# Two layers of AdaLN attention and mixture of experts: the group norm's Newton steps and the decay's affine step change engines in the first attention

## The chip, the cores and the metric

The kernel runs on one core of a Trainium2 chip. The engines that matter here are TensorE (PE in the profile), VectorE (DVE), ScalarE (ACT), GpSimd (POOL) and SyncE (SP), which issues most of the transfers. The metric is the device time of one execution, in microseconds; lower is better. Three runs of the kernel before took 1299.35, 1291.67 and 1298.77 us, so the median is 1298.77.

## The reference, cut to what matters

Two layers work on `x` of 8 sequences, 512 tokens, 128 features. Each layer is `x + ga * attention(h)` and then `x + gb * ffn(h)`, where `h` is a layer norm of `x` with a scale and a shift per sequence. The first layer's attention is a linear recurrence over time with 16 heads of 8 features, and the change lies in it alone:

```python
dd = sigmoid(tanh(einsum('btd,ed->bte', x_shift, ddlerp_w)))
r, k, v = proj(lerp(mix_r), r_w), proj(lerp(mix_k), k_w), proj(lerp(mix_v), v_w)
g = silu(proj(lerp(mix_g), g_w))
w = -softplus(-proj(lerp(mix_w), w_w)) - 0.5
# per step: state = state * exp(w_t) + k_t v_t ;  o_t = sum_v state * r_t
out = _wkv_scan(r, k, v, w)
mu, var = out.mean(-1), out.var(-1)             # over the 8 features of a head
out = (out - mu) / sqrt(var + GN_EPS) * gn_weight + gn_bias
return einsum('btd,ed->bte', out * g, out_w)
```

The decay `exp(w)` is `exp(-0.5) * sigmoid(z)` with `z` the projection, which the kernel computes as `0.5 * exp(-0.5) * (tanh(z/2) + 1)`. The rest (mixture of experts, windowed and global attention, second mixture) is not touched.

## The kernel before

The stage of the first attention works on one sequence at a time, as 128 features x 512 tokens, in a software pipeline. `recurrent_rows` (line 384) runs `step(i)` for i from -3 to 10 on every engine's own queue, with a list of parts written out by hand; in `step(i)` the letters are n = i+3, m = i+2, a = i+1, b = i-1, c = i-2, d = i-3. So in one step sequence i is scanned, sequence i+1 gets its projections, sequence i-1 gets its head norm, output projection and second layer norm, sequence i-2 goes through the shared expert and the router, and i-3 is scattered to the expert slots. Every engine takes its parts strictly in the written order, and semaphores tie the engines together.

**The scan.** For each of the 8 value features j, `unit(b, j)` on DVE multiplies the keys by a row of `vrow` (line 916) and runs the scan with the decay tile `decs[b % 2]` (line 918). `received(b, j)` on POOL multiplies the result with `rrow` (line 1311), and `accumulate(b, j)` on TensorE adds it up, less the head's mean, in PSUM bank 7 (line 1973). `vrow` and `rrow` are values and receptions spread over the partitions: SP stores `vS` (line 482) and `rS` (line 487) to DRAM and loads them back broadcast, 4 MB a sequence (`load_rows`, line 499), in the order units 0 to 3, 6 and 7, 4 and 5. The loads of units 0 to 3 for sequence i+1 wait for both stores and for the accumulation of unit 3 of sequence i. In SP's order `store_reception` and `load_rows` stand behind `load_gate`, which waits for POOL's `gated_shared` (line 1323).

**The head norm.** ScalarE squares and copies bank 7 (lines 1571 and 1572). At the end of step i, `head_variance(i)` on DVE reduces the squares and makes the first guess of the reciprocal root with integer operations on `gnr` (128x64, lines 932 to 935). In step i+1 POOL begins with `head_rsqrt(b)`: three Newton steps of four operations (lines 1336 to 1339), each waiting for the one before by the semaphore `a_gn`. DVE's `head_norm(b)` (line 942) waits for the sixteenth count. It stands behind `unit(i, 0)`, the router of sequence c and `unit(i, 1)`. Then TensorE transposes the heads (`heads_T`, line 1890), ScalarE scales them (`scale_heads`, line 1588), POOL multiplies them with the gate (`gated_y`, line 1349), and TensorE projects (`attended`, lines 2014 and 2020). POOL's own order in a step is `head_rsqrt(b)`, `received(i, 0)`, `scatter` of d (line 1275, four indirect transfers), `gated_out`, `gated_y`, `received` 1 to 3, `gated_shared`, `received` 4 and 5, the second norm's scale, `received` 6, `decay(a)`, `received` 7, `scatter` of c, and the scales of the first and third norm.

**The decay.** ScalarE's `decay(b)` (line 1559) takes the tanh out of bank 2; POOL's `decay(a)` (line 1304) adds 1 and multiplies by `DECAY` in place, for the first `unit` of the next step. On ScalarE the gate's tanh follows (line 1565), then the router's exponential (line 1580), the first modulation (line 1506) and the copy of the attended sequence (line 1592).

ScalarE also issues three transfers: `load_gate`, `load_second` (line 1520, the sequence's residual, which waits for the store of the sequence two before) and `store_second` (line 1525). `load_second` stands ahead of `scale_heads` and of the key's copy (line 1547), which TensorE's next projections need. `keep_busy` (line 1885) is filler on TensorE, around the last sequence.

Of the kernel before, what the change touches and what calls it, by code (L numbers as in the profile page):

```python
# [18 lines left out]
ALU = mybir.AluOpType  # L19
ACT = mybir.ActivationFunctionType  # L20
# [21 lines left out]
DECAY = 0.5 * 0.6065306597126334  # L42
# [16 lines left out]
def build(nc, io):  # L59
    nc.disable_value_cache = True  # L60
    with ExitStack() as ctx:
# [58 lines left out]
        dT, tT, eT, aT_, _, _, vS, kS, dec, gs, tg, y1 = (rows[:, i, :] for i in range(12))  # L120
# [32 lines left out]
        kSs, decs = (kS, late[:, 2, :]), (dec, late[:, 3, :])  # L153
# [16 lines left out]
        gnr = sb("gnr", [P, 3, NT * H])  # L170
# [54 lines left out]
        S = Semaphores()  # L225
# [109 lines left out]
        def ok(b):  # L335

            return 0 <= b < NB

        def half_of(q):

            return q // 2 % 2, q % 2
# [54 lines left out]
        def settled(eng):  # L396

            eng.sem_inc(S["settled"], 1)
# [211 lines left out]
        def _(v):  # L610
            V = nc.vector
# [309 lines left out]
            def head_variance(b):  # L921

                n = [0]

                def link(ins):
                    n[0] += 1
                    ins.then_inc(S["a_gn"], 1)
                    if n[0] < 4:
                        v.wait_ge(S["a_gn"], b * 16 + n[0])
                gv, gy = gnr[:, 0, :], gnr[:, 1, :]  # L930
                v.wait_ge(S["a_sq"], 2 * b + 2)
                link(V.tensor_reduce(gv, sq.rearrange("p (a c) -> p a c", c=DH), axis=AX, op=ALU.add))
                link(V.tensor_scalar(gv, gv, 1.0 / DH, GN_EPS, ALU.mult, ALU.add))
                link(V.tensor_scalar(gy.bitcast(I32), gv.bitcast(I32), 1, None, ALU.logical_shift_right))
                link(V.tensor_scalar(gy.bitcast(I32), gy.bitcast(I32), -1.0, float(RSQRT_MAGIC), ALU.mult, ALU.add))

            def head_norm(b):

                v.wait_ge(S["a_gn"], b * 16 + 16)
                if b:  # L940
                    v.wait_ge(S["a_onT"], b)
                V.tensor_tensor(on.rearrange("p t (h c) -> p (t h) c", c=DH),
                                accS.rearrange("p (a c) -> p a c", c=DH), bc(gnr[:, 1, :], DH, 2), ALU.mult).then_inc(S["a_on"], 1)
# [20 lines left out]
            def step(i):  # L964
                n, m, a, b, c = i + 3, i + 2, i + 1, i - 1, i - 2
                if ok(i):
                    unit(i, 0)
                if ok(c):
                    router(0, c, ROUTE_EPS, 0)
                if ok(i):  # L970
                    unit(i, 1)
                if ok(b):
                    head_norm(b)
                if ok(c):
                    shared_product(c, 0)
                if ok(i):
                    unit(i, 2)
                    unit(i, 3)
                    unit(i, 4)
                    unit(i, 5)  # L980
                if ok(a):
                    gate(a)
                if m == 0:
                    mod_columns()
                    prepare()
                if ok(m):
                    shift(m)
                if ok(b):
                    stats_second(b)
                if ok(c):  # L990
                    router(0, c, ROUTE_EPS, 1)
                if ok(i):
                    unit(i, 6)
                    unit(i, 7)
                if ok(c):
                    place(0, c)
                    shared_product(c, 1)
                if ok(n):
                    stats_first(n)
                if ok(m):  # L1000
                    lerp(m)
                if m == 0:
                    mod_rows()
                    prepare_rest()
                if ok(b):
                    stats_third(b)
                if ok(i):
                    head_variance(i)
# [225 lines left out]
        def _(p):  # L1234
            G_ = nc.gpsimd
# [62 lines left out]
            def norm_second(b):  # L1298
                ln_scale_less("ln2_st", "ln2_rs", b, veps, mv, rstd, nb2)

            def decay(a):
                p.wait_ge(S["a_tz"], a + 1)
                settled(p)
                G_.tensor_scalar(decs[a % 2], decs[a % 2], 1.0, DECAY, ALU.add, ALU.mult).then_inc(S["a_dec"], 1)

            def received(b, j):

                p.wait_ge(S["a_scan"], b * DH + j + 1)
# [13 lines left out]
                    p.wait_ge(S["b_y"], c)  # L1322
                G_.tensor_tensor(swg, wshd[:, :, :], bc(mgd, FC, 1), ALU.mult).then_inc(S["a_swg"], 1)

            def head_rsqrt(b):

                n = [4]

                def link(ins):
                    n[0] += 1  # L1330
                    ins.then_inc(S["a_gn"], 1)
                    p.wait_ge(S["a_gn"], b * 16 + n[0])
                gv, gy, ga_ = gnr[:, 0, :], gnr[:, 1, :], gnr[:, 2, :]
                p.wait_ge(S["a_gn"], b * 16 + 4)
                for _ in range(3):
                    link(G_.tensor_tensor(ga_, gy, gy, ALU.mult))
                    link(G_.tensor_tensor(ga_, ga_, gv, ALU.mult))
                    link(G_.tensor_scalar(ga_, ga_, -0.5, 1.5, ALU.mult, ALU.add))
                    link(G_.tensor_tensor(gy, gy, ga_, ALU.mult))

            def norm_third(b):
                if b:
                    p.wait_ge(S["r_sorted"], b)
# [6 lines left out]

            def step(i):
                n, a, b, c, d = i + 3, i + 1, i - 1, i - 2, i - 3
                if ok(b):
                    head_rsqrt(b)
                if ok(i):
                    received(i, 0)
                if ok(d):
                    scatter(0, d, 1)
                if ok(b):
                    gated_out(b)  # L1360
                    gated_y(b)
                if ok(i):
                    received(i, 1)
                    received(i, 2)
                    received(i, 3)
                if ok(c):
                    gated_shared(c)
                if ok(i):
                    received(i, 4)
                    received(i, 5)  # L1370
                if ok(b):
                    norm_second(b)
                if ok(i):
                    received(i, 6)
                if ok(d):
                    scattered(0, d)
                if ok(a):
                    decay(a)
                if ok(i):
                    received(i, 7)  # L1380
                if ok(c):
                    scatter(0, c, 0)
                if ok(n):
                    norm_first(n)
                if ok(b):
                    norm_third(b)
# [78 lines left out]
        def _(a):  # L1465
            A = nc.scalar
# [88 lines left out]
            def decay(b):  # L1555
                a.wait_ge(S["a_z"], b + 1)
                if b >= 2:
                    a.wait_ge(S["a_scan"], (b - 1) * DH)
                A.activation(decs[b % 2], bank[2][:, :], ACT.Tanh, scale=0.5).then_inc(S["a_tz"], 1)

            def gate_tanh(b):
                a.wait_ge(S["a_g"], b + 1)
# [305 lines left out]
            for q in range(HALVES - 4, HALVES):  # L1868
                p, h = half_of(q)
# [686 lines left out]
```

## Time and profile before

| | us |
|---|---|
| median of three runs | 1298.77 |
| the profiled execution | 1300.29 |
| its span, first to last instruction | 1298.5 |
| TensorE busy | 1151.7 (89%) |
| DVE busy | 834.5 (64%) |
| ScalarE busy | 504.0 (39%) |
| POOL busy | 597.1 (46%) |
| mean granted TensorE clock | 0.943 |

The profile is of one execution. Its time is 1.8 us more than its span and 1.5 us more than the median of the runs. The busy shares are means over stages with different limits. In the order of time: the first attention fills about the first 370 us, then come the first expert blocks, the second attention, and the second expert blocks with the final sum. In the first attention from 36 to 330 us TensorE was busy 229.98 of 294 us, DVE 228.44, POOL 206.45, ScalarE 113.14, with DMA at 68%, so that no engine's total tells the limit there; the order of the waits does. A granted clock of 1.00 is 2.4 GHz on TensorE, 0.50 is 1.2 GHz.

### The profile page before, as it was taken

Reading aid. Unit: us, or ns where it says so; the run is one execution under the profiler, and the core shown is the slowest. Engines: PE = TensorE matmul, PEld = TensorE weight load, DVE = VectorE, ACT = ScalarE, POOL = GpSimd, SP = SyncE. Lnnn points to the kernel's source line nnn. Section 1 sums busy time; section 2 is a strip of 40 time slices with the busy share of each in tenths; the row PEclk is TensorE's granted clock in tenths of the full one; section 3 lists DMA queues with packets and bytes.
Section 4 is the critical chain, followed back from the end, with each engine's and each line's share of the span. In section 5 each row is a group of like instructions: output and inputs, shape, how many; then the busy total and the mean of one; then the engine's idle time right before and its main releaser. Section 6 shows DMA issues by size and latency. Waiting matters only on the chain.

```text
span 1298.5 us, 24171 instructions
## 1 busy us (share of the span) xinstructions
PE 1151.7 (89%) x8163; PEld 774.4 (60%) x8163; DVE 834.5 (64%) x2229; ACT 504.0 (39%) x1147; POOL 597.1 (46%) x701
## 2 busy tenths in 40 slices
PE   6868768887788888899999999999988699999998
PEld 3445436655358886344454454454444599999994
DVE  4778868778434444535659778786776266666664
ACT  3334424443304443033444444434432245454440
POOL 1466867777625555413144454562245133333330
PEclk9889989797979999989999999999988799999999
DMA  4987587563124522101011021110011331111105
GB/s 133 258 207 178 152 255 186 127 169 93 45 67 119 148 82 64 58 27 45 9 50 48 28 59 32 54 38 18 24 40 49 95 103 36 44 38 38 45 20 203
DMA packets 87314, 113.09 MB, mean 87 GB/s; under 512 B 11224, under 2 KB 68888, under 8 KB 84616
## 3 DMA queue, kind: packets, MB, share of 16 engines
q1 hardware_dynamic: 68120, 86.35, 24.6%
q0 software_dynamic: 8640, 17.84, 4.3%
q10 hardware_dynamic: 10432, 7.35, 2.1%
q8 instruction: 67, 1.10, 0.3%
q14 instruction: 55, 0.45, 0.1%
HBM read 81.06 MB, written 32.04 MB: 87 GB/s over the span
## 4 chain that ended last, share of the span: by engine, by line
PE 63%; issue 10%; DVE 9%; DMA 8%; POOL 4%; ACT 4%; SPq 1%; DVEq 1%; ACTq 0%; POOLq 0%; another core or an unknown queue 0%
PE bank L2122 9%; PE bank L2133 8%; PE bank L2235 5%; PE bank L2284 4%; PE bank L2149 3%; PE bank L1885 3%; PE bank L2293 3%; PE bank L2248 3%; DMA region<-vrdram 3%; PE bank L2312 3%; PE bank L2323 2%; PE bank L1973 2%; DMA xres<-rows 1%; PE bank L2308 1%; PE bank L1944 1%
## 5 line engine op out<-in xcount | busy, mean ns | idle before, releaser
L1275 POOL DMA_INDIRECT slots<-pay,slot x128 | 130.4, 1019 | 132.7 <-issue 109.0
L2122 PE MATMUL bank<-rows,wup 128*128 128x128 f32 x1136 | 156.0, 282 | 17.2 <-DVE wup L764 14.0
L1290 POOL DMA_INDIRECT y<-region,xin x78 | 84.2, 1080 | 156.1 <-ACT region L1694 142.1
L2122 PEld LDWEIGHTS bank<-rows,wup 128*128 128x128 f32 x1136 | 142.0, 197 | 21.5 <-issue 10.0
L1794 ACT ACTIVATE w0uv<-bank 128x512 f32<-128x512 f32 x192 | 99.1, 603 | 129.1 <-PE bank L2293 92.6
L2133 PE MATMUL bank<-rows,wse 128*128 128x128 f32 x1136 | 142.1, 278 | 1.7 <-DVE wse L769 1.7
L2133 PEld LDWEIGHTS bank<-rows,wse 128*128 128x128 f32 x1136 | 132.7, 192 | 7.6 <-issue 6.6
L1885 PE MATMUL bank<-consts 128*128 128x512 f32 x240 | 118.9, 633 | 1.9 <-DVE region L1059 1.9
L1037 DVE TENSOR_REDUCE rows<-bank 128x4 f32<-128x512 f32 x128 | 79.5, 684 | 55.3 <-PE bank L2235 55.0
L1290 POOL DMA_INDIRECT y<-hh,region x64 | 68.8, 1075 | 95.4 <-ACT hh L1694 82.2
L757 DVE SCALAR_TENSOR_TENSOR rows<-bank,bcol,rows 128x128 f32<-128x128 f32 x142 | 43.4, 347 | 92.7 <-ACT rows L1683 92.6
L1311 POOL TENSOR_TENSOR region<-region 128x512 f32<-128x512 f32 x64 | 80.9, 1275 | 24.2 <-DVE region L918 22.5
L752 DVE TENSOR_TENSOR rows<-region,bank 128x256 f32<-128x256 f32 x71 | 29.8, 420 | 86.7 <-ACT region L1673 66.2
L1885 PEld LDWEIGHTS bank<-consts 128*128 128x128 f32 x240 | 45.1, 201 | 60.8 <-issue 54.2
L1973 PE MATMUL bank<-consts,region 128*128 128x128 f32 x512 | 70.5, 291 | 3.9 <-POOL region L1311 3.9
L1973 PEld LDWEIGHTS bank<-consts,region 128*128 128x128 f32 x512 | 66.6, 206 | 9.5 <-POOL region L1311 5.1
L1044 DVE TENSOR_REDUCE wam<-bank 128x8 f32<-128x512 f32 x64 | 39.8, 684 | 49.8 <-PE bank L2248 49.8
L1944 PE MATMUL bank<-rows,wam 128*128 128x512 f32 x80 | 46.7, 668 | 21.0 <-ACT wgl L1547 11.6
L916 DVE TENSOR_TENSOR bank<-bank,region 128x512 f32<-128x512 f32 x64 | 44.6, 698 | 22.8 <-DMA region<-vrdram 20.9
L2293 PE MATMUL bank<-rows,pick_g 32*128 32x512 f32 x256 | 53.4, 625 | 0.7 <-ACT rows L1779 0.7
L1677 ACT ACTIVATE region<-bank,bcol 128x128 f32<-128x128 f32 x142 | 44.4, 364 | 19.1 <-PE bank L2133 18.7
L1673 ACT ACTIVATE region<-bank 128x256 f32<-128x256 f32 x71 | 27.3, 384 | 56.5 <-PE bank L2122 46.8
(359 smaller groups left out, 2381.8 us busy)
## 6 DMA issues: line engine op xcount, KB each, us to landing
region<-vrdram SPq DMA_DIRECT2D x16, 1024.0 KB
region<-vrdram SPq DMA_DIRECT2D x32, 512.0 KB
xin<-slots SPq DMA_DIRECT2D x78, 65.0 KB
region<-slots SPq DMA_DIRECT2D x64, 65.0 KB
wgl<-in_wgl SPq DMA_DIRECT2D x8, 512.0 KB
rows<-y SPq DMA_DIRECT2D x8, 512.0 KB, 4.1
wam<-xres SPq DMA_DIRECT2D x9, 256.0 KB, 2.8
xres<-wam SPq DMA_DIRECT2D x9, 256.0 KB, 2.3
```

The costliest lines, as they stand in the source:

```text
L1037: V.tensor_reduce(maxg[:, t, g * QD:g * QD + HG], bank[g].rearrange("p (h k) -> p h k", h=HG), axis=AX, op=ALU.max).then_inc(S["c_mx"], 1)
L1275: p.indirect_dma_start(io["slots"], bass.IndirectOffsetOnAxis(ap=slot_of(l, b)[:, k, t:t + 1], axis=0), pay_of(l, b)[:, k, t, :], None).th ...
L1290: p.indirect_dma_start(io["y"], bass.IndirectOffsetOnAxis(ap=xins[par][:, h, k, P + 1:P + 2].bitcast(U32), axis=0), bYs[par][:, h, k, :], ...
L1311: G_.tensor_tensor(rrow[:, j, :], vrow[:, j, :], rrow[:, j, :], ALU.mult).then_inc(S["a_pr"], 1)
L1794: A.activation(expT[k % 2][:, g, :], bank[g], ACT.Exp, scale=SCALE).then_inc(S["c_exp"], 1)
L1885: M(out, ident, consts[:, 0:T], start=True, stop=True)
L1944: M(out[:, :], wa0[:, w, :], aT_, start=True, stop=False)
L1973: ins = M(bank[7][:, tile(t)], rrow[:, j, tile(t)], center, start=(j == 0 and t == 0), stop=(j == DH - 1 and t == NT - 1), skip_group_chec ...
L2122: ins = M(bank_up(l, n)[:, tile(j)], wup[:, n % 3, tile(j)], bxT[:, q % 2, tile(k)], start=True, stop=True)
L2133: ins = M(bank_second(n)[:, tile(j)], wse[:, n % 2, c, tile(j)], bZ[:, n % 4, c, :], start=c == 0, stop=c == FC - 1)
L2235: M(bank[g], xTs[p][heads(g), tile(t)], gmk[p][heads(g), :, :], start=True, stop=True).then_inc(S["c_S"], 1)
L2293: M(bank[g], pick_g[heads(g), r, :], negmax[heads(g), :], start=False, stop=True).then_inc(S["c_E"], 1)
```

## The change

`head_rsqrt` moves from POOL to DVE. On POOL it stood first in the step; on DVE it stands directly ahead of `head_norm(b)`, behind `unit(i, 1)`. Each Newton step now has three operations in place of four: the product with the variance and the factor -0.5 are one `scalar_tensor_tensor`, and so are the addition of 1.5 and the product with the guess. The semaphore `a_gn` counts 13 a sequence in place of 16. The decay's addition and product move from POOL to ScalarE, as an activation `Copy` with scale and bias `DECAY`, directly behind the tanh, for which it waits. The arithmetic is otherwise the same, and no transfer is touched.

```diff
-                        v.wait_ge(S["a_gn"], b * 16 + n[0])
+                        v.wait_ge(S["a_gn"], b * 13 + n[0])
...
+            def head_rsqrt(b):
+                n = [4]
+                def link(ins):
+                    n[0] += 1
+                    ins.then_inc(S["a_gn"], 1)
+                    v.wait_ge(S["a_gn"], b * 13 + n[0])
+                gv, gy, ga_ = gnr[:, 0, :], gnr[:, 1, :], gnr[:, 2, :]
+                v.wait_ge(S["a_gn"], b * 13 + 4)
+                for _ in range(3):
+                    link(V.tensor_tensor(ga_, gy, gy, ALU.mult))
+                    link(V.scalar_tensor_tensor(out=ga_, in0=ga_, scalar=-0.5, in1=gv, op0=ALU.mult, op1=ALU.mult))
+                    link(V.scalar_tensor_tensor(out=gy, in0=ga_, scalar=1.5, in1=gy, op0=ALU.add, op1=ALU.mult))
...
-                v.wait_ge(S["a_gn"], b * 16 + 16)
+                v.wait_ge(S["a_gn"], b * 13 + 13)
...
                 if ok(b):
+                    head_rsqrt(b)
                     head_norm(b)
...
-            def decay(a):
-                p.wait_ge(S["a_tz"], a + 1)
-                settled(p)
-                G_.tensor_scalar(decs[a % 2], decs[a % 2], 1.0, DECAY, ALU.add, ALU.mult).then_inc(S["a_dec"], 1)
...
-            def head_rsqrt(b):
-                for _ in range(3):
-                    link(G_.tensor_tensor(ga_, gy, gy, ALU.mult))
-                    link(G_.tensor_tensor(ga_, ga_, gv, ALU.mult))
-                    link(G_.tensor_scalar(ga_, ga_, -0.5, 1.5, ALU.mult, ALU.add))
-                    link(G_.tensor_tensor(gy, gy, ga_, ALU.mult))
...
                 A.activation(decs[b % 2], bank[2][:, :], ACT.Tanh, scale=0.5).then_inc(S["a_tz"], 1)
+                a.wait_ge(S["a_tz"], b + 1)
+                A.activation(decs[b % 2], decs[b % 2], ACT.Copy, scale=DECAY, bias=DECAY).then_inc(S["a_dec"], 1)
```

## Rows read from the trace of the kernel before

**Rows 1.** Busy time by stretch. Columns: us, busy per engine (x instructions), clock, DMA share, GB/s

```profile
100.00:140.00 40.00, 32.36 (x158) 20.64 (x157) 35.58 (x110) 17.53 (x32) 27.16 (x44) 1.00 0.84 198
220.00:260.00 40.00, 33.35 (x150) 22.81 (x149) 30.30 (x81) 15.30 (x26) 29.28 (x43) 0.83 0.62 160
229.00:239.00 10.00, 8.36 (x19) 4.69 (x20) 5.76 (x7) 4.19 (x8) 8.23 (x8) 0.51 0.20 66
```

**Rows 2.** Chain of waits, 36 to 104 us. Columns: start, us, what

```profile
75.24 0.59 DVE wgl L942
...
85.13 2.69 PE bank L1973 x24
...
88.47 11.60 DMA region<-vrdram
```

**Rows 3.** Chain of waits, 0 to 345 us

```profile
168.88 19.02 DMA xres<-rows
...
215.78 12.28 DMA xres<-x
```

**Rows 4.** Waits of SP's queue, 36 to 330 us. Columns: total us, times, longest

```profile
SPq L398 <- POOL rows L1323: 102.4, 6, 21.4
```

**Rows 5.** POOL in order of time. Columns: start, us, instruction, idle before it

```profile
136.18 0.29 POOL L1336 TENSOR_TENSOR gnr<-gnr 128x64 f32<-128x64 f32 x1
...
140.39 0.32 POOL L1339 TENSOR_TENSOR gnr<-gnr 128x64 f32<-128x64 f32 x1
...
140.79 1.78 POOL L1311 TENSOR_TENSOR region<-region 128x512 f32<-128x512 f32 x1
...
148.05 1.27 POOL L1349 TENSOR_TENSOR rows<-rows 128x512 f32<-128x512 f32 x1
```

**Rows 6.** Tile gnr on DVE. Columns: ns min/median/max, first and last start

```profile
L933 DVE TENSOR_SCALAR gnr<-gnr x8: 195/196/382, 63.4 to 319.9; 128x64 f32<-128x64 f32 x8
...
L942 DVE TENSOR_TENSOR wgl<-wgl,gnr x8: 666/691/1568, 75.2 to 328.8; 128x512 f32<-128x512 f32 x8
```

**Rows 7.** Groups of DVE, 60 to 330 us. Columns: busy us, mean ns, idle before

```profile
L897 DVE SCALAR_TENSOR_TENSOR rows<-rows,hT 128x512 f32<-128x512 f32 x6 | 4.1, 692 | 0.2
...
L701 DVE TENSOR_TENSOR oh<-oh,pos 128x32 f32<-128x32 f32 x12 | 2.3, 192 | 0.4
```

**Rows 8.** DVE in order of time

```profile
132.82 0.70 DVE L916 TENSOR_TENSOR bank<-bank,region 128x512 f32<-128x512 f32 x1
...
140.74 0.69 DVE L942 TENSOR_TENSOR wgl<-wgl,gnr 128x512 f32<-128x512 f32 x1
...
170.55 0.70 DVE L916 TENSOR_TENSOR bank<-bank,region 128x512 f32<-128x512 f32 x1 [1.31 <-DMA region<-vrdram]
...
298.15 0.67 DVE L942 TENSOR_TENSOR wgl<-wgl,gnr 128x512 f32<-128x512 f32 x1
...
328.82 0.69 DVE L942 TENSOR_TENSOR wgl<-wgl,gnr 128x512 f32<-128x512 f32 x1 [1.48 <-POOL gnr L1339]
```

**Rows 9.** ScalarE in order of time

```profile
142.41 0.78 ACT L1588 ACTIVATE rows<-bank,gnv 128x512 f32<-128x512 f32 x1 [4.12 <-PE bank L1890]
...
205.03 0.60 ACT L1529 ACTIVATE rows<-bank 128x512 f32<-128x512 f32 x1 [4.09 <-PE bank L1940]
...
205.66 0.63 ACT L1531 ACTIVATE rows<-rows 128x512 f32<-128x512 f32 x1
...
238.98 0.60 ACT L1592 ACTIVATE x<-bank 128x512 f32<-128x512 f32 x1 [1.92 <-PE bank L2020]
```

**Rows 10.** TensorE in order of time

```profile
229.95 2.07 PE L1944 MATMUL bank<-rows,wam 128*128 128x512 f32 x2 [3.97 <-ACT rows L1547]
...
332.96 2.59 PE L1885 MATMUL bank<-consts 128*128 128x512 f32 x4
...
336.37 1.13 PE L2020 MATMUL bank<-owg,rows 128*128 128x128 f32 x8 [0.82 <-POOL rows L1349]
```

**Rows 11.** Line 1304, the decay's affine step on POOL

```profile
L1304 POOL TENSOR_SCALAR rows<-rows x4: 617/617/619, 29.8 to 245.5; 128x512 f32<-128x512 f32 x4
```

More of the change, by code:

```diff
@@ L1323, in gated_shared @@
                 G_.tensor_tensor(swg, wshd[:, :, :], bc(mgd, FC, 1), ALU.mult).then_inc(S["a_swg"], 1)
-            def head_rsqrt(b):
[L1327 to L1334, printed above, removed]
-                for _ in range(3):
-                    link(G_.tensor_tensor(ga_, gy, gy, ALU.mult))
-                    link(G_.tensor_tensor(ga_, ga_, gv, ALU.mult))
-                    link(G_.tensor_scalar(ga_, ga_, -0.5, 1.5, ALU.mult, ALU.add))
-                    link(G_.tensor_tensor(gy, gy, ga_, ALU.mult))
             def norm_third(b):
@@ L1352, in step @@
                 n, a, b, c, d = i + 3, i + 1, i - 1, i - 2, i - 3
-                if ok(b):
-                    head_rsqrt(b)
                 if ok(i):
@@ L1376, in step @@
                     scattered(0, d)
-                if ok(a):
-                    decay(a)
                 if ok(i):
```

## The prediction

> **What bounds the kernel now.** I read the profile from the coarse to the fine. The stretches of equal length come first, because the change touches the recurrent first attention alone: nothing of it runs after the eighth sequence's head norm, at 328.82 us [rows 8]. In the first of the two long stretches DVE is busy 35.58 of 40 us while POOL is at 27.16 and ACT at 17.53; in the second DVE is down to 30.30 and TensorE's granted clock to 0.83 [rows 1]. So the stage has no single bound: some steps are held by DVE, others by something else. Then the chain of waits, for what that something is. Early it runs through DVE, TensorE and the reload of `vrow` and `rrow` from DRAM: head norm at 75.24, the accumulations for units 1 to 3 at 85.13, then 11.60 us of loads [rows 2]. Later it runs through two long stores of the residual stream, 19.02 and 12.28 us [rows 3]: they queue among those loads, and ScalarE stands behind them, since its reload of the next sequence waits for the store. Last, the waits of SP's own queue: 102.4 us in six waits on the POOL operation of L1323, `gated_shared` [rows 4]. SP reaches a sequence's second store and its loads only after that, so POOL's place in its order sets when they may start.
>
> **The Newton steps leave POOL.** The first of the twelve links starts at 136.18 and the last ends at 140.39 + 0.32 = 140.71 [rows 5]: 4.5 us of POOL per sequence, 36 us in eight. The next operation, the product of unit 0, starts at 140.79 [rows 5], so POOL wasn't waiting for it.
>
> **They come to DVE.** Nine operations on 128x64. No row shows a two-tensor operation of 64 columns on DVE in this stage. It is bounded below by the one-source form on the same tile, 196 ns [rows 6], and above by the 512-column `scalar_tensor_tensor`, 692 ns [rows 7]. The 32-column `tensor_tensor` takes 192 ns [rows 7], so the low end is much the nearer; 480 columns more cost 500 ns, 32 more about 33. I take 192 + 33 = 225 ns, plus an estimated 30 ns to the next link, which waits for it: 9 x 0.255 = 2.3 us a sequence. The ends are 9 x 0.20 = 1.8 and 9 x 0.72 = 6.5 us; over the three steps that pay, below, they would change the sum by -1.5 and +12.6, and the 32-column row leaves almost nothing of the second. Over all sequences 18.4 us come to DVE.
>
> What counts is where they lie. DVE works in order, so they no longer run while DVE waits for its loads: they stand after units 0 and 1, directly ahead of head norm, and TensorE's head transposes, with everything queued behind them (the decay projection, the residual projection, the accumulations 1 to 4), wait for head norm.
>
> Step i of the loop scans sequence i and normalises sequence i-1.
> - Step 0: no Newton steps. 0.
> - Step 1: POOL used to be done before DVE's loads landed, and head norm starts at 75.24 as unit 1 ends, on the chain [rows 2]. **+2.3**.
> - Step 2: DVE is busy from end to end [rows 1], and unit 0 of sequence 3 starts at 132.82 with no idle time before it [rows 8]. **+2.3**.
> - Step 3: here POOL is late. Its gated product of the heads starts at 148.05, behind four scatters, behind the Newton steps [rows 5]. Without them POOL would be ready 4.6 us earlier (4.5 and a gap); but the product also needs ScalarE's scaled heads, which start at 142.41, 1.67 us after head norm at 140.74 [rows 8, 9]. Head norm goes 2.3 us later, so scaled heads end about 145.5, and the product starts there: 2.5 us earlier. Units 1 to 3 on POOL, L1323, SP's store and the loads of sequence 4 follow. DVE, 2.3 us longer, is then the one that is late for unit 0 of sequence 4: it waited 1.31 us for loads [rows 8], so that start moves by +1.0. But what ends step 4 is the store behind the loads [rows 3], and that goes with the loads: **-2.5**.
> - Steps 4, 5 and 6: the loads and the store that drains with them decide [rows 3]. DVE's 2.3 us lie under them: TensorE stands idle 3.97 us before the key projection at 229.95 [rows 10]. **0**. If that cover were gone, each would cost 2.3.
> - Step 7: head norm at 298.15 follows unit 1, and DVE then works on without a gap. **+2.3**.
> - Step 8: head norm waits 1.48 us for POOL [rows 8]. On DVE the steps start after the router, about 327.3, and end at 329.6: 0.8 late. POOL's scatters run 4.5 us earlier, so its product no longer comes last; TensorE's filler matmuls, begun at 332.96 and 2.59 us long, do, where before it waited 0.82 us more for POOL [rows 10]. Filler that starts 0.8 later ends as the wait did. **0**.
>
> **The decay's affine step.** POOL loses 617 ns a sequence [rows 11]. ScalarE gains a second activation that waits for the first; such a pair starts 0.63 us apart (205.03 and 205.66) [rows 9], so 0.63 us a sequence, 5 us in all. Behind it stand the gate's tanh, the router's exponential and the copy of the attended sequence. That copy, at 238.98, is preceded by 1.92 us of idle time, until TensorE [rows 9]; I put the step at **0**, and its upper bound is 0.63 x 8 = 5.0 if that idle time isn't there in other steps. Below zero nothing, since a POOL that waits loses nothing. No DMA is moved; the scan's wait on the decay stays satisfied early, since sequence i+1 is prepared in step i.
>
> **A rule to weigh: the shared port.** Head norm, two inputs in SBUF, takes between 666 and 1568 ns [rows 6], 0.9 us longer where POOL's product overlaps it. POOL's unit 0 product will now fall on DVE's router or Newton operations instead of on head norm; I count it as moved, not added: 0, with 0.9 a sequence as its upper end. The Trainium skill, "SBUF — State Buffer", section "SBUF: two separate sides", says that a DVE operation with two SBUF inputs and a POOL operation that reads SBUF hold the port pair exclusively, the loser blocked for the whole instruction. By that rule each of the nine new operations on DVE has such a partner to meet. This is rival 3.
>
> **Sum:** 2.3 + 2.3 - 2.5 + 0 + 2.3 + 0 = +4.4 us. The profiled execution took 1300.29 us, 1.8 beyond its span; 1304.7 after. It lies 1.5 us above the median shown (1298.77), so the median should be about **1303**.
>
> **The rivals.**
> 1. *The cover isn't there: DVE pays in full (slower).* Place: the DVE stretches of steps 4 to 6. It decides once DVE's own idle time there is under 2.3 us a step. For it: 35.58 of 40 us busy, unit 0 of sequence 3 unhindered. Against it: 30.30 of 40 later [rows 1]. All eight sequences at 2.3 and nothing given back are 18.4; 1300.3 + 18.4 - 1.5 = 1317. Chance 7%.
> 2. *TensorE's clock (faster).* At 229.95 the engine came out of 3.97 us of idleness, and from 229 to 239 it was granted 0.51, the lower level, 1.2 GHz, with 8.36 us of work in ten [rows 1, 10]. Head transposes 1.5 to 2.3 us later fall into that idle time and shorten it. If 2.4 GHz then stays in steps 4, 5 and 7, each gives back up to half of 8.4, 4.2 us: 4.4 - 12.6 = -8.2, a median of 1291. The opposite is possible in steps 1 and 2, where idle time grows. Chance 22%. Only with step 3's gain larger as well does it pass 1%.
> 3. *The port.* A Newton or router operation blocked in each of the steps on the path (1, 2, 3, 7) in addition to what head norm pays now: 4 x 0.9 = 3.6, so 1307; with a whole POOL product of 1.27 us [rows 5] each, 4 x 1.27 = 5.1, so 1308. Chance 15%. That a whole product is waited for is what the skill's page says; the 0.9 is what the rows show.
> 4. *The affine step comes through* (the copy of the attended sequence is late): up to 5.0, so 1308. Chance 8%. A table load with it is unlikely: ScalarE's order has copies between tanhs already.
> 5. *It does less than it says:* the fused operations take nearer 0.3 us, 2.7 a step, so three times 0.4 more: 1304. It lies inside the forecast's own range and chance.
>
> **The numbers.** The forecast holds 48%, its own range 1299 to 1308. Rivals 3 and 4 lie just above, rival 2 below. The range that leaves out 2 in 10 reaches from 1291, where the clock helps in three steps, to 1311: **1291 to 1311**. A measurement of this kernel can't tell less than about 1%, 13 us, from no change. Slower by over 1% is over 1311.8: rival 1 and a sum of 3 and 4 with a lost clock, 9%. Faster by over 1%, under 1285.8, needs rival 2 in every step and more: 7%. Within 1%: 84%.
>
> **What would show it.** Nine DVE operations of about 225 ns between unit 1 and head norm; POOL's product of unit 0 directly after the third norm; head norm 2.3 us further from unit 0 in steps 1, 2 and 7; the gated product at step 3 some 2.5 us sooner behind unit 0; the store of 19.02 us down to some 15, since it is issued later behind loads that began sooner; the clock in the ten microseconds after the ScalarE wait at 0.5 again. I am wrong if the last head norm, at 328.82 [rows 8], comes less than 1 or more than 9 us later (4.4 + 0.8 = 5.2 by the sum), or if the granted clock before the loads of steps 4 to 7 differs.

## The result and the profile after

| | us |
|---|---|
| the kernel before, median of 15 runs | 1293.46 |
| the changed kernel, median of 15 runs | 1301.62 |
| ratio, with its 95% interval | 1.0067 [1.0045, 1.0089] |
| the profiled execution of the changed kernel | 1299.81 |
| its span | 1298.0 |

The change costs 0.67%, 8.7 us on 1293.46 (5.8 to 11.5). That is within 1% and inside the range, and 1301.62 is near the forecast of 1303, but by two errors that nearly cancel, which is luck: the three runs shown ahead of the prediction had a median 5.3 us above that of the fifteen, and the change cost 8.7 us where 4.4 were forecast. A second measurement, beside e10 to e12 below, gave 1.0061 [1.0038, 1.0084]. The prediction held that less than 1% can't be told from no change; with this many runs the interval is 0.22% either way.

Ratios here and below are of the fast runs, and three of e4's twelve runs (1292.39 to 1300.01 us, at granted clocks of 0.943 to 0.948) were slow and are not in its ratio. A ratio is not the quotient of the two medians, and can differ from it by up to 0.2%: the medians above differ by 8.2 us. Amounts in us are worked out from the ratios.

The two profiled executions differ by 0.5 us (1300.29 and 1299.81), since that of before lies 6.8 us above its median. So the total of one profile can't carry this result; the order of events inside the first attention can, with some care: a single profile's last head norm is uncertain by some microseconds, as e1 will show.

The profile's page, engines of the changed kernel (busy us, share of the span, instructions):

```profile
PE 1150.1 (89%) x8163; PEld 776.0 (60%) x8163; DVE 852.0 (66%) x2301; ACT 508.9 (39%) x1155; POOL 564.8 (44%) x597
```

DVE has its 72 new instructions and 17.5 us more, ScalarE 8 and 4.9 us, POOL 104 and 32.3 us less. The stretches that answer to [rows 1]:

```profile
100.00:140.00 40.00, 32.19 (x151) 22.54 (x150) 34.92 (x98) 15.93 (x28) 19.94 (x23) 0.87 0.72 164
220.00:260.00 40.00, 32.93 (x148) 22.06 (x146) 32.08 (x88) 17.03 (x30) 24.46 (x30) 0.83 0.59 158
229.00:239.00 10.00, 5.58 (x17) 2.79 (x18) 9.49 (x14) 2.13 (x4) 5.62 (x6) 0.66 0.27 88
```

POOL fell from 27.16 to 19.94 us in the first stretch, and the granted clock from 1.00 to 0.87: TensorE stood idle there behind a later head norm (0.87 us busy of the six from 106 us, 3.53 before). From 100 to 330 us as a whole the clock averages 0.89 before and 0.90 after.

Tile `gnr` on DVE, answering to [rows 6] (ns min/median/max, first and last start), and who waited for it:

```profile
L948 DVE TENSOR_TENSOR gnr<-gnr x24: 199/225/360, 75.1 to 334.5; 128x64 f32<-128x64 f32 x24
L949 DVE SCALAR_TENSOR_TENSOR gnr<-gnr x24: 224/225/226, 75.4 to 334.7; 128x64 f32<-128x64 f32 x24
L950 DVE SCALAR_TENSOR_TENSOR gnr<-gnr x24: 224/225/360, 75.6 to 335.0; 128x64 f32<-128x64 f32 x24
...
L957 DVE TENSOR_TENSOR wgl<-wgl,gnr x8: 691/692/966, 77.5 to 335.3; 128x512 f32<-128x512 f32 x8
...
  PE bank L1883: 34.2, 7
```

Each new operation takes the 225 ns of the forecast, and head norm no longer meets POOL's product for long (966 ns at most, 1568 before). DVE in step 3 in order of time, answering to [rows 8]:

```profile
138.28 0.70 DVE L916 TENSOR_TENSOR bank<-bank,region 128x512 f32<-128x512 f32 x1
...
141.66 0.19 DVE L642 TENSOR_TENSOR lg<-bank,wgl 128x32 f32<-128x32 f32 x1 [1.43 <-POOL wgl L1259]
141.88 1.06 DVE L643 TENSOR_TENSOR lg<-lg,rbias 128x32 f32<-128x32 f32 x1
...
147.03 0.20 DVE L948 TENSOR_TENSOR gnr<-gnr 128x64 f32<-128x64 f32 x1
...
149.22 0.23 DVE L950 SCALAR_TENSOR_TENSOR gnr<-gnr 128x64 f32<-128x64 f32 x1
149.54 0.69 DVE L957 TENSOR_TENSOR wgl<-wgl,gnr 128x512 f32<-128x512 f32 x1
```

and POOL beside it, answering to [rows 5]:

```profile
141.63 1.26 POOL L1322 TENSOR_TENSOR region<-region 128x512 f32<-128x512 f32 x1
...
152.27 1.27 POOL L1344 TENSOR_TENSOR rows<-rows 128x512 f32<-128x512 f32 x1 [3.43 <-ACT rows L1581]
```

Two things are to be seen. The Newton steps run from 147.03 to 149.45, 2.4 us between unit 1 and head norm. And DVE had been idle for 1.43 us just before, waiting for POOL's scale (L1259), work that they could have covered but stand behind; the router's next operation, with two inputs in SBUF, then took 1.06 us for 0.19, to the end of POOL's product of unit 0, which had begun 0.25 us ahead of it. Before, the Newton steps stood on POOL between its scale and this product. L643 is slow in four steps, 3, 4, 5 and 7, and among the steps with a scan these are the four in which DVE had waited for the scale. POOL, freed, waits 3.43 us for ScalarE's scaled heads. The chain of waits, answering to [rows 2] and [rows 3]:

```profile
86.47 2.69 PE bank L1966 x24
89.81 11.74 DMA region<-vrdram
...
128.55 1.24 DVE dcur L694
...
175.95 16.23 DMA xres<-rows
...
219.47 12.92 DMA xres<-x
```

`dcur`, line 694, is new here. It is the update of the running destination in the token placement `place` (`tensor_scalar`, 128x8), directly behind scan 7. SP's queue waits as before, answering to [rows 4]:

```profile
SPq L398 <- POOL rows L1334: 99.3, 6, 21.9
```

The lag of the changed profile behind that of before, in us, by step:

| | 1 | 2 | 3 | 4 | 5 | 6 | 7 | 8 |
|---|---|---|---|---|---|---|---|---|
| unit 0 of the step | 0.0 | +1.5 | +5.5 | +6.5 | +3.9 | +4.1 | +2.9 | |
| head norm | +2.4 | +4.1 | +8.8 | +10.8 | +7.8 | +6.3 | +5.9 | +6.5 |
| forecast, head norm | +2.3 | +4.6 | +6.9 | | | | | +5.2 |

### The profile page after: what moved, and what is told of

It is laid out like the page before. It is cut to its first block, busy times and chain, and to the rows that moved or that the text cites. A ratio compares the mean times of both kernels' runs of the same rounds, so it can differ in the third digit from the quotient of the medians.

```text
span 1298.0 us, 24133 instructions
## 1 busy us (share of the span) xinstructions
PE 1150.1 (89%) x8163; PEld 776.0 (60%) x8163; DVE 852.0 (66%) x2301; ACT 508.9 (39%) x1155; POOL 564.8 (44%) x597
## 4 chain that ended last, share of the span: by engine, by line
PE 63%; DVE 10%; issue 9%; DMA 8%; ACT 4%; POOL 3%; SPq 1%; DVEq 0%; ACTq 0%; POOLq 0%
PE bank L2126 9%; PE bank L2115 9%; PE bank L2228 5%; PE bank L2142 4%; PE bank L2277 4%; PE bank L1878 3%; PE bank L2286 3%; PE bank L2241 3%; DMA region<-vrdram 3%; PE bank L2305 3%; PE bank L2316 3%; DVE region L918 2%; DMA vrdram<-wgl 2%; PE bank L1966 1%; POOL slots L1291 1%
## 5 line engine op out<-in xcount | busy, mean ns | idle before, releaser
L2115 PEld LDWEIGHTS bank<-rows,wup 128*128 128x128 f32 x1136 | 140.8, 195 | 19.6 <-issue 10.6
L916 DVE TENSOR_TENSOR bank<-bank,region 128x512 f32<-128x512 f32 x64 | 44.7, 698 | 16.7 <-DMA region<-vrdram 14.8
L769 DVE COPY wse<-wgl 128x1024 f32 x71 | 48.8, 689 | 0.1
```

The costliest lines, as they stand in the source:

```text
L2115: ins = M(bank_up(l, n)[:, tile(j)], wup[:, n % 3, tile(j)], bxT[:, q % 2, tile(k)], start=True, stop=True)
```

## The experiments

Every run was taken in the same manner, with the kernel before run beside it. The first four kernels ran where before takes 1294 us, e5 to e8 on a second chip, where it takes 1259.74, and e9 to e12 on a third, where it takes 1261.35; so the ratio is what is compared, and "last head norm" only on one chip. e9 repeats the change beside e10 to e12. The kernel before has a profile on the first chip alone.

### e1: the Newton steps alone

```diff
 # the change, with the decay's affine step back on POOL
+                if ok(a):
+                    decay(a)
                 if ok(i):
                     received(i, 7)
```

> The change without its second part: the Newton steps on DVE in nine operations, the decay's affine step back on POOL. Forecast (the affine step lies under ScalarE's idle time, cost 0): as slow as the whole change, ratio to the kernel before about 1.006, last head norm in the profile 6 us later than before. Rival 4 (the affine step comes through): about 4 us of the 8.7 are gone, ratio near 1.003.

Measured: 1299.66 us, ratio 1.0042 [1.0021, 1.0063], +5.4 us. The move of the Newton steps costs about what the sum gave for the whole change (+4.4); the ratio lies between the forecast of this run (1.006) and rival 4's 1.003. Its last head norm, 338.10 us, is 9.3 us later than before, where 6 was expected, and 2.8 later than in the change, which is the slower kernel by its runs. The profiled execution took 1304.27 us, 4.6 above e1's median. So a lag read from a single profile can be off by some 3 us, and the ratios decide.

### e2: the affine step alone

```diff
 # the kernel before, with POOL's decay(a) removed
                 A.activation(decs[b % 2], bank[2][:, :], ACT.Tanh, scale=0.5).then_inc(S["a_tz"], 1)
+                a.wait_ge(S["a_tz"], b + 1)
+                A.activation(decs[b % 2], decs[b % 2], ACT.Copy, scale=DECAY, bias=DECAY).then_inc(S["a_dec"], 1)
```

> The kernel before with only the affine step moved to ScalarE. Forecast: ratio 1.000 (0 to +1 us), last head norm within 1 us of 328.8. Rival 4: +3 to +5 us, ratio 1.003 to 1.004, with the gate's tanh and the copy of the attended sequence 0.6 us later in each step and nothing absorbing it.

Measured: 1297.34 us, ratio 1.0045 [1.0025, 1.0064], +5.8 us, last head norm 331.94 (328.82 before). The quotient of the medians is lower, 1.0025, and gives 3.2 us. The prediction put this step at 0. ScalarE has room for it: four of its copies of the attended sequence still wait 7.4 us in all for TensorE from 60 to 330 us (8.3 before). The trace shows something else. Behind scan 7 of sequence 2, the kernel before, DVE and POOL together:

```profile
123.52 0.62 POOL L1304 TENSOR_SCALAR wgl<-wgl 128x512 f32<-128x512 f32 x1
...
123.99 0.18 DVE L693 CAST pay<-dcur 128x8 uint32<-128x8 f32 x1
124.20 0.17 DVE L694 TENSOR_SCALAR dcur<-dcur 128x8 f32<-128x8 f32 x1
124.22 1.28 POOL L1311 TENSOR_TENSOR region<-region 128x512 f32<-128x512 f32 x1
```

and e2:

```profile
125.83 0.15 DVE L693 CAST pay<-dcur 128x8 uint32<-128x8 f32 x1
125.99 1.27 POOL L1306 TENSOR_TENSOR region<-region 128x512 f32<-128x512 f32 x1 [0.71 <-DVE pay L693]
126.01 1.28 DVE L694 TENSOR_SCALAR dcur<-dcur 128x8 f32<-128x8 f32 x1
```

Before, POOL's decay ran from 123.52 to 124.14 and kept the product of unit 7 back, so the update of `dcur` began 0.02 us ahead of it and took 0.17 us. Without the decay the product begins 0.02 us ahead of the update, which takes 1.28 us, the product's whole length. Before, two of the stage's six updates were slow (0.63 and 1.27 us); in e2, e4 and the change all six are:

```profile
L694 DVE TENSOR_SCALAR dcur<-dcur x6: 1268/1272/1279, 128.5 to 319.6; 128x8 f32<-128x8 f32 x6
```

(line 694 of the changed kernel.) In e1, which keeps the decay on POOL, one of six is. That is 1.1 us of DVE a step, and of everything behind it in `place`. Head norm met POOL's product more often too, at 1.16 to 1.56 us in four steps for two before. The Trainium skill, "SBUF — State Buffer", section "SBUF: two separate sides", has it that whichever of POOL's operation and a DVE operation that needs the shared ports starts first keeps them for its whole length. The trace agrees: 1.28 us against 1.27.

### e3: six Newton steps in place of three, on DVE

```diff
-                for _ in range(3):
+                for _ in range(6):
```

> The whole change with six Newton steps on DVE in place of three: nine more operations, 2.3 us a sequence, at the same place (the result converges after three, so the output stays the same). Forecast: steps 4, 5 and 6 stay covered by the transfers, the others pay, so +7 to +12 us on the change, ratio to the kernel before 1.012 to 1.016. Rival 1 (no cover): 8 x 2.3 = 18.4 us more, ratio 1.021.

Measured: 1319.44 us, ratio 1.0209 [1.0176, 1.0243]; against the change's 1.0067 that is +1.4%, 18 us, plus or minus 5. Expected were 7 to 12; all eight sequences at 2.3 us give 18.4. Its profile has the last head norm at 350.1 us, 14.8 later than the change. Of these, 10.5 us had come by step 4, only 1.5 more by step 7 and 2.8 in step 8. So more of the second helping of 2.3 us is paid than of the first, and the first four steps pay it in full; that every step does isn't shown. DVE's waits from 60 to 330 us show where the cover went (total us, times, longest), before:

```profile
DVE bank L916 <- DMA region<-vrdram: 15.6, 5, 7.2
DVE wgl L904 <- ACT rows L1565: 7.3, 1, 7.3
DVE lg L642 <- POOL wgl L1243: 5.6, 3, 3.6
```

the change:

```profile
DVE bank L916 <- DMA region<-vrdram: 10.6, 3, 7.5
DVE lg L642 <- POOL wgl L1259: 5.0, 4, 1.4
...
DVE wgl L904 <- ACT rows L1558: 1.7, 1, 1.7
```

and e3:

```profile
DVE bank L916 <- DMA region<-vrdram: 12.0, 3, 7.4
DVE lg L642 <- POOL wgl L1259: 5.0, 4, 1.8
```

The change had used up most of the waits that lie behind head norm (L904: 7.3 to 1.7 us), and in e3 that one is gone. What is left in e3 are waits for loads and for POOL's scale, which stand ahead of the Newton steps in DVE's order and can't be filled by them.

### e4: the Newton steps at the end of the step before

```diff
                     head_variance(i)
+                    head_rsqrt(i)
...
                 if ok(b):
-                    head_rsqrt(b)
                     head_norm(b)
```

> The whole change with the nine operations of sequence i moved to the end of step i, directly behind head_variance, ahead of the next unit 0 instead of behind unit 1. If what costs is that they stand behind the loads, between unit 1 and head norm: DVE's idle time before unit 0 (2.1, 1.3 and 3.5 us in steps 2, 4 and 7, and more in steps 1 and 8) takes them in, and POOL's release in step 3 counts in full: ratio 0.996 to 1.000, last head norm at 323 to 328 us. If DVE's time costs wherever it stands: ratio 1.006 as the change.

Measured: 1285.74 us, ratio 0.9929 [0.9899, 0.9959], 9.2 us less than before and 18 less than the change, plus or minus 5, with the same nine operations on the same engine. That is more than was expected (0.996 to 1.000), and so is the last head norm, 318.80 us for 323 to 328. DVE in step 3:

```profile
136.81 0.22 DVE L950 SCALAR_TENSOR_TENSOR gnr<-gnr 128x64 f32<-128x64 f32 x1
137.07 0.70 DVE L916 TENSOR_TENSOR bank<-bank,region 128x512 f32<-128x512 f32 x1
137.81 1.22 DVE L918 TENSOR_TENSOR_SCAN region<-wgl,bank 128x512 f32<-128x512 f32 x1
138.94 0.17 DVE L642 TENSOR_TENSOR lg<-bank,wgl 128x32 f32<-128x32 f32 x1
139.14 0.19 DVE L643 TENSOR_TENSOR lg<-lg,rbias 128x32 f32<-128x32 f32 x1
```

and its waits from 60 to 330 us:

```profile
DVE bank L916 <- DMA region<-vrdram: 6.6, 2, 5.6
...
DVE lg L642 <- POOL wgl L1259: 1.1, 1, 1.1
```

Ahead of unit 0 the Newton steps fill the time in which DVE waits for its loads (10.6 to 6.6 us) and for POOL's scale (5.0 to 1.1). The router then finds its scale ready (no idle time before L642), and L643 takes 0.19 us. The gain isn't DVE's alone: from 100 to 330 us TensorE's granted clock is 0.93 for 0.89 before, and over the runs in the ratio it averages 0.955 for 0.947 (e10: 0.952 for 0.948). That is rival 2's direction, and no run separates the clock's share from the rest.

### e5: e2, with the update of `dcur` last in `place`

```diff
                 link(V.tensor_copy(pay_of(layer, b)[:, :, :, P + 1].bitcast(U32), dcur[:, :, :]))
-                link(V.tensor_scalar(dcur[:, :, :], dcur[:, :, :], 2.0 * T, None, ALU.add))
...
                 link(V.tensor_copy(slot_of(layer, b)[:, :, :], slotf[:, :, :]))
+                link(V.tensor_scalar(dcur[:, :, :], dcur[:, :, :], 2.0 * T, None, ALU.add))
```

> The kernel before with the decay's affine step on ScalarE, as in e2, and with one more edit: in `place` on VectorE the update of the running destination (dcur, 128x8) is the last of the twelve small operations, no longer the second, directly behind scan 7. Theory A (the port): in e2 POOL's product of unit 7 begins at the end of scan 7, where the decay had stood before it, and all six updates of dcur wait for it (1.27 us for 0.17 us). Moved away from there the updates should take 0.17 us, the last head norm should fall from 331.94 us back to 327 to 329.5, and the ratio to before from 1.0045 to 0.998 to 1.001. Theory B (ScalarE's queue): the affine step costs by what it puts off on ScalarE, the exponentials and copies behind it; then the edit gives nothing, the last head norm stays at 331 to 333 us and the ratio at 1.003 to 1.006.

Measured: 1257.07 us, ratio 0.9978 [0.9952, 1.0005]. In the trace the update no longer waits and the four additions behind it pass POOL's product unhindered:

```profile
125.61 1.27 POOL L1306 TENSOR_TENSOR region<-region 128x512 f32<-128x512 f32 x1 [0.71 <-DVE pay L693]
```

That was POOL in order of time, and this is DVE:

```profile
125.64 0.75 DVE L696 TENSOR_TENSOR base<-base,bank 128x8 f32<-128x8 f32 x4
...
127.65 0.17 DVE L703 CAST slot<-slotf 128x8 uint32<-128x8 f32 x1
127.85 0.17 DVE L705 TENSOR_SCALAR dcur<-dcur 128x8 f32<-128x8 f32 x1
```

The slots are ready 3.3 us behind the start of scan 7 (124.31 to 127.65), 4.6 in e2 (124.69 to 129.25), and POOL's scatter starts a microsecond sooner. The ratio is just under theory A's range, and its interval excludes theory B's. How much of it is the repaired wait, e11 has to tell.

### e6: the change, with `dcur` last

> The change, with the update of dcur as the last operation of `place` instead of the second. Theory A (the port takes about 1.1 us of VectorE in each of the six steps that place tokens): last head norm from 335.32 us to 329 to 332, ratio to before 1.001 to 1.004, the copy and updates of dcur at 0.15 to 0.2 us each. Theory B (all of the loss is VectorE's Newton steps, and the port's waits fall on time that VectorE had free anyway): last head norm stays at 334 to 336 us, ratio 1.005 to 1.009.

Measured: 1266.5 us, ratio 1.0044 [1.0021, 1.0066], last head norm 331.84; e9, the change on the third chip, has 1.0061 and 333.57. The gain of 0.17% has an interval of about 0.3% either way: it lies between the two theories' ranges and decides for neither. The router's L643, blocked for 0.87 us in four steps of the change, was still blocked in three here.

### e7: e4, with `dcur` last

> The change with the Newton steps directly behind the head variance at the end of a step (as in e4), and the update of dcur last in `place`. Theory A: 5 to 6 us less than e4 in the stage, last head norm 313 to 316 us, ratio to before 0.987 to 0.991. Theory B (the waits at the port lie on time that VectorE has free): as e4, last head norm 318 to 320 us, ratio 0.992 to 0.995.

Measured: 1256.72 us, ratio 0.9957 [0.993, 0.9983]. The last head norm is at 327.88, in neither theory's range; those were worked out from e4, on the first chip. The reference is e10, the same kernel as e4 on the third chip, with 326.27.

### e8: e4, with the decay's affine step on POOL

> Newton steps on VectorE directly behind the head variance, the decay's affine step still on POOL (so the change's first half, placed early). Theory A: the decay on POOL stands between the products of units 6 and 7, so dcur's update gets the port first (0.17 us in at least four of six), and the kernel is 3 to 6 us shorter than e4: ratio to before 0.988 to 0.991. Theory B (moving the affine step is neutral or helps, because POOL is the one that is late): ratio 0.993 to 0.996, no better than e4.

Measured: 1255.23 us, ratio 0.9962 [0.9937, 0.9988], with one of the stage's updates of `dcur` at 1.27 us and the rest at 0.17. The ratio is in theory B's range, but its interval reaches into theory A's.

### e9: the change once more

> The change itself, run once more beside the next three kernels, so that its profile and ratio stand beside theirs from one chip. All theories: the ratio to before within the interval of the first measurement, 1.0045 to 1.0089, the last head norm 5 to 8 us behind that of the kernel before on the same kind of chip, and all six updates of dcur at 1.27 to 1.28 us.

Measured: 1269.87 us, ratio 1.0061 [1.0038, 1.0084]; all six updates between 1.269 and 1.280 us. The last head norm is at 333.57; how far that is behind the kernel before on this chip isn't known.

### e10: e4 once more

> The same kernel as e4, for comparison with the change, e7 and e8 on one kind of chip. If the port's waits cost what they take (theory A), e7 and e8, which have lost them, should be 3 to 6 us shorter than this one, so it should read 0.998 to 1.001 where they read 0.996. If those waits lie on time that VectorE has free once its Newton steps are early (theory B), it reads 0.993 to 0.997, as they do.

Measured: 1257.95 us, ratio 0.9971 [0.9945, 0.9997]. e7 and e8, on the second chip, are 0.14% and 0.09% below it, with about 0.37% of uncertainty. That is nearer theory B: the six updates of `dcur` behind a scan are slow here (1.27 us), in e7 none, and it can't be told in the time. But theory A's 3 to 6 us are 0.24% to 0.48%, within that uncertainty. With the Newton steps early, no cost of the port's waits or of the affine step's place could be measured, and one of up to 0.5% isn't excluded.

### e11: the kernel before, with `dcur` last

> The kernel before with only the update of dcur moved to the end of `place`. In the profile of before two of six updates waited for the port (0.63 and 1.27 us for 0.17), so theory A gives some 1.5 us less, ratio 0.997 to 1.000; theory B gives no difference, 0.999 to 1.001. What matters is that it is not as large as the 0.7% between e2 and e5.

Measured: 1258.45 us, ratio 0.9967 [0.9945, 0.999]. This is 4 us, with an interval of 1.3 to 6.9, where the profile of before had 1.5 us of slow updates. The edit may give something by itself, by earlier slots and scatters as the trace of e5 has them, but 1.5 us isn't excluded. Of the 0.67% between e2 and e5, half appears here without the affine step having been moved. Against e11, the affine step on ScalarE (e5) costs 0.9978 / 0.9967 = 1.0011, plus or minus 0.35%; without the edit (e2) it cost 1.0045. That points to the port as the place of its cost, but the difference, 0.34% with 0.40% of uncertainty, doesn't prove it.

### e12: POOL's release by itself

```diff
 # the kernel before; two of three Newton steps on POOL left out
-                for _ in range(3):
+                for _ in range(1):
```

> The kernel before with one Newton step of three on POOL: it leaves out two Newton steps of the group norm's inverse root, so POOL's chain is eight operations (about 2.5 us) shorter and nothing is added to VectorE. It prices POOL's release by itself. Forecast of the prediction: POOL's release counts in step 3 alone (the gated product waits for POOL there) and comes to some 2 us: last head norm 326 to 328 us, ratio 0.997 to 0.9995. Rival, the release is worth it in each of the eight steps: 0.986 to 0.990. Rival, nothing: ratio 0.9995 to 1.0015. From this and e1 the price of the nine operations on VectorE follows as the difference.

Measured: 1258.39 us, ratio 0.997 [0.9943, 0.9998], 3.8 us less than before. It takes 8 of 12 links from POOL and gives nothing to DVE. It isn't POOL's release quite alone: in its profile head norm takes 0.67 us in all eight steps, where before it took 1.56 in two, so DVE is blocked for less time too.

## Why the prediction was right, and where it wasn't

**The cost of the nine operations: right.** Per operation 225 ns were forecast, 225 measured; head norm came 2.35 us later in step 1, where 2.3 was the term.

**POOL's release: not contradicted.** The sum had -2.5 us, in step 3 alone. e12 measured -3.8 us, plus or minus 3.5, for two thirds of the links; the 13 to 18 us of a release that counts in each step are excluded. That it counts in step 3 alone isn't shown.

**DVE's share, three steps of eight: about right.** e1 pays for DVE and has the release, e12 has most of the release only: 5.4 + 3.8 = 9.2 us, four steps at 2.3, with 4.4 us of uncertainty. The sum had three, 6.9. The table shows where they fell. From unit 0 to head norm of the same step the lag grew in every step from 1 to 7, by 2.4, 2.6, 3.3, 4.3, 3.9, 2.2 and 3.0 us. What steps 4, 5 and 6 added was given back by the next unit 0 (lags of 3.9, 4.1 and 2.9), behind the loads and the store, as the cover of the forecast has it. Step 7 kept its 3.0 (2.3 forecast), and in step 8 head norm's lag grew by 0.6 (0.8 forecast). Rival 1 (all eight, 18.4) didn't happen; e3 shows that the cover doesn't reach much further.

**Step 3: the step that went wrong first.** Head norm was to be 6.9 us late and was 8.8; the product of the heads on POOL was to start 2.5 us sooner behind unit 0 and started 1.2 us sooner (14.0 us behind it, 15.2 before). ScalarE's scaled heads, which the prediction had named as the cap, came 9.0 us later with head norm. Two DVE operations that waited for POOL's products account for the 1.9 us in size: 1.1 us at `dcur` in step 2, on the chain at 128.55, and 0.87 us at L643 in step 3. The store that follows was issued 7.1 us later than before and ended 4.3 us later, since it took 16.23 us in place of 19.02; the forecast was "some 15" and a net +2.1. That its end moves less than its issue was right.

**The decay's affine step at 0: wrong.** This is the term that failed. It was argued from ScalarE's room, and "a POOL that waits loses nothing" was used to say that POOL's order doesn't matter. e2 measured +5.8 us (3.2 to 8.3), about the upper bound of 5.0. On the change, e1 gives the same step as 1.0067 - 1.0042 = 0.25%, 3.2 us, with 3.9 us of uncertainty. The mechanism that the profile points to isn't rival 4's (a late copy of the attended sequence) but rival 3's: taking 0.62 us out of POOL's order between the products of units 6 and 7 gave the product of unit 7 the ports ahead of a DVE operation that used to come first; in both traces the two starts lie 0.02 us apart.

**The port "moved, not added": right for the Newton steps, wrong for the affine step.** From 60 to 330 us, counted over the shortest duration of each operation, head norm was blocked for 1.9 us before and 0.1 after, the router's sum L656 for 1.3 and 0, and L886, the difference of the shifted tokens (128x512), for 4.5 and 2.6. Against that L643 went from 0.1 to 3.5, the nine new operations have 1.0, and the update of `dcur` went from 1.6 to 6.6. Over all of DVE's instructions there it is 13.7 us before and 17.2 after, 3.5 more. In e1, which moves the Newton steps alone, it is 10.9, less than before, and in e2 19.2. So the 5.4 us of e1 aren't blocked time that was added; what was added is `dcur`, and it came with the affine step. The prediction weighed the port for POOL's product of unit 0 alone.

How much of the change's cost this is stays open. The rival's 3.6 to 5.1 us on top of 4.4 would make 8.0 to 9.5, and 8.7 was measured, but that fit proves nothing: e6 has all six updates at 0.17 us and 9.7 us of blocked time, 4 less than before, and still costs 1.0044, a gain of 0.17% on e9 with 0.32% of uncertainty. e11 gained 0.33% from the same edit, so with `dcur` last on both sides the change is still 1.0044 / 0.9967 = 1.0077, plus or minus 0.32%. The change isn't slower than before by line 694 alone: by e1, 5.4 of its 8.7 us come with the Newton steps.

**TensorE's clock: it moved, and the mean stayed.** The lower level came between 108 and 135 us, where before had none. TensorE had been busy for 0.35 of the four microseconds from 106 us, and from 110 to 116 it was granted 0.50; it had been busy for 2.00 of the four from 126, and from 130 to 133 it was granted 0.50 again:

```profile
108.00:118.00 10.00, 5.83 (x18) 3.91 (x19) 9.35 (x19) 2.15 (x4) 4.83 (x5) 0.66 0.55 136
118.00:129.00 11.00, 9.63 (x64) 7.53 (x62) 9.91 (x23) 7.57 (x13) 7.04 (x10) 1.00 0.41 101
129.00:135.00 6.00, 5.37 (x28) 4.89 (x29) 5.41 (x22) 2.77 (x6) 2.58 (x3) 0.72 1.03 218
```

(the changed kernel, columns as in [rows 1]). From 229 to 239 us there was less of it, 0.66 for 0.51, and from 290 to 300 none, 1.00 for 0.50. The prediction had called itself wrong if the clock ahead of the loads of steps 4 to 7 differed, and by that sign it was, though its other sign held (the last head norm 6.5 us later, between 1 and 9). Both directions are in rival 2, and in the mean they cancel: over 100 to 330 us it is 0.90 for 0.89. The clock's share can't be separated from the run-to-run spread.

**What the prediction didn't ask.** Whether DVE has room is one question; where in its order is another. It found that DVE waits for its loads and for POOL's scale, and that the nine operations stand behind those waits, but didn't price the other place. That place is worth 18 us on the first chip (1.0067 to 0.9929) and 11 on the third (1.0061 to 0.9971), clock included, more than any term of the sum.

By these runs the best kernel is e4, with or without the edit of e7 or e8: 0.993 of the time before on the first chip, 0.996 to 0.997 on the other two.

## What to carry to other kernels

Work that is moved onto an engine in order should go where that engine waits, ahead of the operation whose inputs come late, as soon as its own input is there; the same change cost 8 to 9 us with the nine operations directly ahead of their user, and gained 4 to 9 us with them at the end of the step before. When an operation is taken out of POOL's order, look at what moves up: here a POOL product that then started with the end of a DVE scan made a small DVE operation behind it wait for the whole product. And count the base as well as the effect: three runs put it 5 us too high, more than the sum.

## What the runs showed of the hardware that wasn't expected

- A `tensor_scalar` of 128x8 on DVE took 1.28 us in place of 0.17 when a POOL product of 1.27 us had begun 0.02 us earlier. Just behind it, `tensor_tensor` operations with one input in PSUM ran at their usual pace under such a product (four in 0.75 us in e5), as did L642 (0.19 us) in the change, whereas L643, with both inputs in SBUF, took 1.06 us for 0.19.
- `tensor_tensor` and `scalar_tensor_tensor` of 64 columns took the same 225 ns on DVE (medians). By that, fusing twelve operations to nine saves as many operations' time; twelve unfused ones were not run there.
- The same kernel before took 1294 us on one chip and 1260 us on two others. At least part of it is in a later stage: TensorE's idle time before the experts' up projection (released by DVE's L764) is 17.0 us in the profile of e4 on the first chip, and none shows in that of e10, the same kernel on the third. Up to the last head norm e10 is the later of the two, 326.27 us for 318.80. What makes the difference wasn't tried.
